# High and low parts in the MLP stages, and a reciprocal one step later, in an eight-stage transformer kernel

## The chip, the cores and the metric

The kernel runs on one core of one Trainium2 chip. The metric is the device time of one execution in microseconds, as the median of several executions.

## The reference

The reference is a chain of four transformer layers on x of 8 batches x 512 tokens x 256 features, with a second tensor (the context) of the same size. The kernel runs it as eight stages: causal self-attention, cross-attention and MLP (layer 0), cross-attention (layer 1), masked self-attention, cross-attention and MLP (layer 2), and causal attention with 64-wide heads (layer 3). The change touches the two MLPs and, by a step, the five attention stages with 16 heads of 16.

```
h = _ln(x, ln3_g, ln3_b)
h = jax.nn.gelu(_lin(h, fc_w, fc_b), approximate=False)   # 256 -> 1024
x = x + _lin(h, proj_w, proj_b)                           # 1024 -> 256
...
q = q.reshape(B, T, NUM_HEADS, HEAD_DIM)                  # attention, 16 heads of 16
scores = jnp.einsum('bqhd,bkhd->bhqk', q, k) * SCALE
probs = jax.nn.softmax(scores, axis=-1)
out = jnp.einsum('bhqk,bkhd->bqhd', probs, v).reshape(B, T, C)
```

All inputs and outputs are float32.

## The kernel before

The five engines each have a program of their own, written out by hand; they meet only in semaphores. x stays in SBUF as X, 128 tokens x 256 features per tile, four tiles for each of the eight batches. The stages run in the order SELF0, CROSS0, MLP0, CROSS1, SELF2, CROSS2, MLP2, SELF3.

**An MLP stage** (mlp(s) on each engine) goes over the eight batches. VectorE takes the statistics of the next batch's rows (layer_norm_x), and GpSimd makes the normalised rows XH from them (rows_scale, rows_centre, rows_times: four instructions) and later adds the output bias to X (add_bias). TensorE turns XH into the PSUM banks LA and LB (turn), and ScalarE moves them with scale and shift into hT (turned): features on partitions, 512 tokens. Then TensorE makes the eight chunks of 128 hidden features, each from two products (c = 0, 1) of a 128x128 piece of the first weights with hT (512 columns), in the four banks FR (the banks MX and ST in the trace). ScalarE puts each through Gelu into h1T (shown as V). After the eighth, TensorE turns the next batch, and then makes the output: for each of four tiles of 128 tokens, eight products of a 128x128 piece of h1T with 256 columns of the second weights, in the banks OV. VectorE adds these to X (add_to_x). All matmul operands of the MLP are plain float32; the trace has two records for each such matmul. The middle six batches are a hardware loop (Fori).

**The attention stages** go over 16 units each (a unit is a batch with 8 of the 16 heads). A unit is 8 steps i of 4 sub-steps j, written out in run_slots and slot. In each sub-step TensorE makes one tile of the row maxima of the next unit (max_tile, in the banks MX0, MX1 and OV1) and one tile of the scores of this unit (score_tile). Their operands come from stk, which already holds high and low parts of q and k in the type float32r, the rounded form that TensorE takes in one pass; each such matmul has one record. VectorE reduces each tile of maxima, in order, and frees its bank (mx_red). ScalarE makes the exponentials (exp_tile). A stage with a mask (SELF2) goes by GpSimd and VectorE too (add_mask), and ScalarE's exponential of such a tile follows a step later (late_exp); there, GpSimd multiplies the outputs between the masks of step 4 and step 5.

The sums of the softmax come with the outputs of attention. They are moved by DMA from ovs to the small tile few; VectorE inverts them (invert, line 1181, called at line 1137); two more DMAs, which SyncE issues in spread_rows and widen, spread the result over sums; and GpSimd multiplies the outputs by it (line 1470). project_out on TensorE waits for that, in every second unit, at step (6, 2). These are the lines that hold the reciprocal's place:

```
if at == ((2, 3) if lagged(s, u) else (1, 3)) and on["tail"]:
    invert(U, 1 - half)
```

lagged is true for the units of SELF2 and for the first unit that follows it.

In the trace, a line number of a helper stands for all its callers: L527 is every matmul, L537 every turn of XH, L1106 add_to_x, L993 Gelu, L987 turned, L1087 and L1094 the statistics.

## Time and profile before

| | |
|---|---|
| median of 3 runs | 4442.07 us (4435.71 to 4443.62) |
| profiled execution, its own time | 4439.38 us |
| its span, from first to last instruction | 4437.7 us |
| mean granted TensorE clock | 0.936 |
| the two MLP stages | about 1178 to 1422 us and 3113 to 3357 us of the span |

An instruction's record runs from its start to its end. Records of TensorE overlap, because matmuls are pipelined, so the pace of a series is read from the distance between starts, not from the length of one record. "Idle before" is the time in which the engine had nothing to do ahead of the instruction, with the engine and line that ended it.

### The profile page before, as it was taken

To read this page: it belongs to the slowest core of one execution; us is meant where nothing else is said; L and a number is where in the kernel's file an instruction comes from. 1 tells how busy PE (TensorE), PEld (TensorE's weight loads), DVE (VectorE), ACT (ScalarE), POOL (GpSimd) and SP (SyncE) were. 2 spreads that over 40 slices of the span, in tenths; PEclk is the share of its full clock that TensorE was granted. 3 is DMA by queue.
4 is the path that set the end of the run, shared out by engine and by line. 5 is a ranking of instruction groups with operands and counts; after the bars stand their busy time and mean duration, and the time that the engine had idled before them with its cause. 6 is when DMAs were issued, how large, how long until landed. Compare 5 with 4: busy or idle time off the path is not lost. (4 is left out here: it accounts for less than half of the span.)

```text
span 4437.7 us, 63144 instructions
## 1 busy us (share of the span) xinstructions
PE 4074.3 (92%) x19794; PEld 1951.2 (44%) x19794; DVE 2527.6 (57%) x6511; ACT 2391.1 (54%) x5045; POOL 1643.8 (37%) x1661
## 2 busy tenths in 40 slices
PE   6888899999797899999999999998897999999998
PEld 2333333333365333333333333333564555555555
DVE  4555557777102677778999977774102444444443
ACT  2444446666321466667788876665222555555553
POOL 2323321111122111126777632111223666666664
PEclk7888889999799799998999999997998999999999
DMA  4333334443000444434333344432000000000000
GB/s 97 82 60 61 64 63 91 80 77 71 23 0 10 65 103 80 74 70 79 61 59 65 59 89 80 78 74 42 20 0 29 6 11 1 11 11 11 11 6 10
DMA packets 135468, 219.92 MB, mean 50 GB/s; under 512 B 42736, under 2 KB 45168, under 8 KB 133488
## 3 DMA queue, kind: packets, MB, share of 16 engines
q1 hardware_dynamic: 135152, 216.02, 24.9%
q8 instruction: 160, 2.62, 0.3%
q14 instruction: 156, 1.28, 0.1%
HBM read 59.69 MB, written 5.51 MB: 15 GB/s over the span
## 5 line engine op out<-in xcount | busy, mean ns | idle before, releaser
L962 ACT ACTIVATE Pr<-ST 128x512 f32<-128x512 f32 (+3 forms) x2220 | 1161.2, 560 | 895.6 <-PE ST L527 881.4
L527 PE MATMUL ST<-stk 50*128 50x512 f32 (+3 forms) x2560 | 1029.0, 464 | 105.3 <-ACT Pr L962 71.8
L1167 DVE TENSOR_REDUCE mx<-MX 128x1 f32<-128x512 f32 x1056 | 699.1, 683 | 233.2 <-PE MX L527 232.5
L527 PE MATMUL MX<-stk 48*128 48x512 f32 (+3 forms) x1760 | 740.2, 458 | 24.4 <-issue 11.8
L1545 POOL TENSOR_SCALAR Pr<-Pr,mx 128x128 f32<-128x128 f32 (+3 forms) x512 | 549.1, 1085 | 386.0 <-DVE mx L1307 386.0
L527 PE MATMUL OV<-Pr,V 128*32 128x512 f32 (+3 forms) x4784 | 646.6, 615 | 2.6 <-ACT Pr L962 1.5
L527 PEld LDWEIGHTS MX<-stk 48*128 48x128 f32 x1760 | 316.7, 194 | 569.6 <-DVE mx L1167 231.3
L527 PEld LDWEIGHTS ST<-stk 50*128 50x128 f32 x2560 | 428.8, 194 | 285.8 <-ACT Pr L962 205.4
L1418 POOL CAST mhl<-mx 128x16 fp32r<-128x16 f32 x160 | 31.6, 198 | 1100.4 <-DVE mx L1167 1055.0
L527 PE MATMUL OV<-stk 48*128 48x512 f32 (+3 forms) x800 | 364.5, 456 | 58.8 <-DVE mx L1167 44.3
L1167 DVE TENSOR_REDUCE mx<-OV 128x1 f32<-128x512 f32 x480 | 324.7, 676 | 54.7 <-PE OV L527 53.4
L527 PEld LDWEIGHTS OV<-stk 48*128 48x128 f32 x800 | 156.5, 196 | 333.5 <-DVE mx L1167 221.3
L1034 ACT ACTIVATE Pr<-MX,mx 128x128 f32<-128x128 f32 (+3 forms) x256 | 135.1, 528 | 265.1 <-DVE mx L1301 264.7
L1164 DVE CUSTOM_DVE_ANT_0 MX<-MX,later 128x128 f32<-128x128 f32 (+3 forms) x352 | 174.1, 511 | 174.4 <-PE MX L527 171.9
L1415 POOL TENSOR_TENSOR X<-X,brow 128x1024 f32<-128x1024 f32 (+1 forms) x56 | 132.2, 2361 | 378.3 <-DVE X L1106 378.3
L1106 DVE TENSOR_TENSOR X<-OV,X 128x512 f32 (+1 forms) x32 | 22.1, 691 | 428.0 <-PE OV L527 428.0
L1160 DVE CUSTOM_DVE_ANT_0 MX<-MX,W_even 128x512 f32<-128x512 f32 x352 | 242.8, 699 | 32.3 <-PE MX L527 30.2
L1316 DVE COPY PT<-OV 128x128 f32<-128x128 f32 (+3 forms) x256 | 125.6, 491 | 227.7 <-PE OV L809 227.7
L1496 POOL TENSOR_TENSOR Pr<-Pr,W_odd 128x512 f32<-128x512 f32 x172 | 219.8, 1281 | 88.6 <-ACT Pr L962 88.2
L1301 DVE CUSTOM_DVE_ANT_0 MX<-MX,sums 128x128 f32<-128x128 f32 (+3 forms) x256 | 126.9, 496 | 212.7 <-PE ST L527 207.5
L527 PE MATMUL OV<-W_even,V 128*128 128x256 f32 x1024 | 225.2, 381 | 1.6 <-ACT V L993 1.6
L1503 POOL TENSOR_SCALAR_AFFINE_SELECT Pr<-Pr 128x512 f32<-128x512 f32 x128 | 81.4, 636 | 381.6 <-ACT Pr L962 381.6
(141 smaller groups left out, 7230.9 us busy)
## 6 DMA issues: line engine op xcount, KB each, us to landing
stk<-hi SPq DMA_DIRECT2D x640, 128.0 KB, 4.2
stk<-lo SPq DMA_DIRECT2D x320, 128.0 KB, 4.0
misc<-misc SPq DMA_DIRECT2D x160, 128.0 KB
sums<-spread SPq DMA_DIRECT2D x80, 256.0 KB
misc<-in_ctx_t SPq DMA_DIRECT2D x24, 512.0 KB, 6.5
W_even<-in_w SPq DMA_DIRECT2D x4, 1024.0 KB, 5.0
W_even<-in_w SPq DMA_DIRECT2D x2, 2048.0 KB, 10.0
XH<-in_ctx_rows SPq DMA_DIRECT2D x8, 512.0 KB, 3.9
```

Of the source, the lines that this page charges most:

```text
L527: return nc.tensor.matmul(o, l, r, start=start, stop=stop)
L962: nc.scalar.activation(pr_buffer(s, u, i)[:, h, q0:S], ST[h % 2][:, q0:S], ACT.Copy if addmask else ACT.Exp).then_inc(ex_done, 2 if addmas ...
L1034: nc.scalar.activation(P3(qt, h)[:, 0:k_n], S3[h][t % 2][:, 0:k_n], ACT.Exp, bias=low3[:, qt, h:h + 1], scale=-1.0, accum_out=total3[:, qt ...
L1160: nc.vector.tensor_tensor_reduce(bank[:, :], bank[:, :], mask_q[:, qt, :], 1.0, -3.0e38, ALU.add, ALU.max, m).then_inc(mx_red, 1)
L1164: nc.vector.tensor_tensor_reduce(bank[:, 0:k_n], bank[:, 0:k_n], later0[:, S - k_n:S], 1.0, -3.0e38, ALU.add, ALU.max, m).then_inc(mx_red, 1)
L1167: nc.vector.tensor_reduce(m, bank[:, :], AX.X, ALU.max).then_inc(mx_red, 1)
L1301: nc.vector.tensor_tensor_reduce(bank, bank, later3[:, S - k_n:S], 1.0, 3.0e38, ALU.add, ALU.min, low3[:, qt, h:h + 1]).then_inc(low3_done, 1)
L1316: nc.vector.tensor_copy(to, TP3[1][:, 0:P * (qt + 1)].rearrange("p (k n) -> p k n", n=P)).then_inc(tp3_evac[1], 1)
L1415: nc.gpsimd.tensor_tensor(xt(b, 0, NT), xt(b, 0, NT), bias, ALU.add).then_inc(x_done, 1)
L1496: nc.gpsimd.tensor_tensor(tile, tile, mask_k[:, i % 4, :], ALU.add).then_inc(pool_masked, 1)
L1503: nc.gpsimd.affine_select(tile, tile, [[0, G], [1, P]], ALU.is_ge, 0.0, 0, -1).then_inc(cleared, 1)
L1545: nc.gpsimd.tensor_scalar(tile, tile, inv3[:, qt, h:h + 1], None, ALU.mult).then_inc(nm3_done, 1)
```

## The change

In both MLP stages each matmul operand is held as a high part (the float32 value rounded to float32r) and a low part (the rest), and each product is made as three: high by high, low weight by high, and high weight by low. ScalarE cuts the weights' high parts in eight pieces at the head of the stage (split_weights) and VectorE the low ones (weights_low). ScalarE writes the turned rows twice, as hi and as hT, and VectorE subtracts them into lo (low_turned). VectorE makes h1_hi and h1_lo from each Gelu chunk (split_hidden). The eight batches are written out, with no loop. In VectorE's queue of the attention stages the reciprocal stands one step later: after sub-step (2, 3) in place of (1, 3), and after (3, 3) in place of (2, 3) where lagged holds. The new tiles lie on SBUF that the MLP stages don't use otherwise (stk, misc, Pr). GpSimd's part of the MLP does the same work as before, without the loop.

```diff
+        w_hi = stk[:, 16:24, :].rearrange("p a n -> p (a n)")
+        w_lo = stk[:, 24:32, :].rearrange("p a n -> p (a n)")
+        misc_at, pr_at = hot + 4 * 18432, hot + 4 * 26624
+        h1_hi = nc.alloc_sbuf_tensor_at("h1_hi", [P, NF, S], F32R, offset=misc_at)
+        h1_lo = nc.alloc_sbuf_tensor_at("h1_lo", [P, NF, S], F32R, offset=pr_at)
...
 
             return W[s % 2][:, 512 * m:512 * m + 512].rearrange("p (c o) -> p c o", c=NC)
 
+
+        def weight_cut(k):
+
+            if k < 4:
+                return [(E * k + c * 1024, E) for c in range(NC)]
+            return [(2048 + 512 * (k - 4), 512)]
+
+        def w_part(w, cut):
+
+            at, n = cut[0]
+            if len(cut) == 2:
+                return w[:, 0:2048].rearrange("p (c o) -> p c o", c=NC)[:, :, at:at + n]
+            return w[:, at:at + n]
 
         def stages(u):
 
...
 
             def mlp(s):
                 m = MLP_NO[s]
-                wf = W[s % 2][:, 0:2048].rearrange("p (c o) -> p c o", c=NC)
-                wp = W[s % 2][:, 2048:4096].rearrange("p (f o) -> p f o", f=NF)
+                wf_hi, wf_lo = (w[:, 0:2048].rearrange("p (c o) -> p c o", c=NC) for w in (w_hi, w_lo))
+                wp_hi, wp_lo = (w[:, 2048:4096].rearrange("p (f o) -> p f o", f=NF) for w in (w_hi, w_lo))
 
                 def turn(b):
                     MB = NB * m + b
...
                         wait(pe, ml_evac, 2 * (MB - 1) + c + 1)
                         transpose_x(s, b, c, bank).then_inc(ml_full, 1)
 
-                def batch(b, more):
+                def batch(b):
                     MB = NB * m + b
-                    pe.wait_ge(ml_evac, 2 * (MB + 1))
+                    pe.wait_ge(ml_hi, 2 * (MB + 1))
                     for f in range(NF):
+                        cut = slice(P * f, P * f + P)
                         wait(pe, gelu_done, NF * MB + f - 3)
+                        if b == 0 and f % 2 == 0:
+                            pe.wait_ge(wf_hi_done, 8 * m + f // 2 + 1)
+                            pe.wait_ge(wf_lo_done, 8 * m + f // 2 + 1)
                         for c in range(NC):
-                            last = mm(FR[f % 4][:, :], wf[:, c, P * f:P * f + P], hT[:, c, :], c == 0, c == NC - 1)
+                            mm(FR[f % 4][:, :], wf_hi[:, c, cut], hi[:, c, :], c == 0, False)
+                            mm(FR[f % 4][:, :], wf_lo[:, c, cut], hi[:, c, :], False, False)
+                        if f == 0:
+                            pe.wait_ge(ml_lo, 2 * (MB + 1))
+                        for c in range(NC):
+                            last = mm(FR[f % 4][:, :], wf_hi[:, c, cut], lo[:, c, :], False, c == NC - 1)
                         last.then_inc(fc_full, 1)
-                    if more:
+                    if b + 1 < NB:
                         turn(b + 1)
-                    pe.wait_ge(gelu_done, NF * (MB + 1))
+                    if b == 0:
+                        pe.wait_ge(wf_hi_done, 8 * (m + 1))
+                        pe.wait_ge(wf_lo_done, 8 * (m + 1))
                     for j in range(2):
                         wait(pe, pr_evac, 2 * (MB - 1) + j + 1)
                         for t in range(2):
-                            tok = slice(P * (2 * j + t), P * (2 * j + t) + P)
+                            tok, bank = slice(P * (2 * j + t), P * (2 * j + t) + P), OV[j][:, E * t:E * t + E]
                             for f in range(NF):
-                                last = mm(OV[j][:, E * t:E * t + E], h1T[:, f, tok], wp[:, f, :], f == 0, f == NF - 1)
+                                if j == 0 and t == 0:
+                                    pe.wait_ge(h1_hi_done, NF * MB + f + 1)
+                                mm(bank, h1_hi[:, f, tok], wp_hi[:, f, :], f == 0, False)
+                                mm(bank, h1_hi[:, f, tok], wp_lo[:, f, :], False, False)
+                            for f in range(NF):
+                                if j == 0 and t == 0:
+                                    pe.wait_ge(h1_lo_done, NF * MB + f + 1)
+                                last = mm(bank, h1_lo[:, f, tok], wp_hi[:, f, :], False, f == NF - 1)
                         last.then_inc(pr_full, 1)
 
                 turn(0)
-                batch(0, True)
-                with pe.Fori(1, NB - 1) as b:
-                    batch(b, True)
-                batch(NB - 1, False)
+                for b in range(NB):
+                    batch(b)
 
             def layer3(s):
                 w_q = W[1][:, 0:2048].rearrange("p (c o) -> p c o", c=NC)
...
             def mlp(s):
                 m = MLP_NO[s]
 
+                def split_weights():
+
+                    act.wait_ge(w_in[s], 16)
+                    for k in range(8):
+                        cut = weight_cut(k)
+                        nc.scalar.activation(w_part(w_hi, cut), w_part(W[s % 2], cut), ACT.Copy).then_inc(wf_hi_done, 1)
+
                 def turned(b):
+                    MB = NB * m + b
                     for c, bank in enumerate((LA, LB)):
-                        act.wait_ge(ml_full, 2 * (NB * m + b) + c + 1)
+                        act.wait_ge(ml_full, 2 * MB + c + 1)
+                        nc.scalar.activation(hi[:, c, :], bank[:, :], ACT.Identity, **scale_shift(s, c)).then_inc(ml_hi, 1)
                         nc.scalar.activation(hT[:, c, :], bank[:, :], ACT.Identity, **scale_shift(s, c)).then_inc(ml_evac, 1)
 
-                def batch(b, more):
+                def batch(b):
                     for f in range(NF):
                         at = C_F + NF * m + f
                         act.wait_ge(fc_full, NF * (NB * m + b) + f + 1)
                         nc.scalar.activation(h1T[:, f, :], FR[f % 4][:, :], ACT.Gelu,
                                              bias=cols[:, at:at + 1]).then_inc(gelu_done, 1)
-                    if more:
+                    if b + 1 < NB:
                         turned(b + 1)
 
+                split_weights()
                 turned(0)
-                batch(0, True)
-                with act.Fori(1, NB - 1) as b:
-                    batch(b, True)
-                batch(NB - 1, False)
+                for b in range(NB):
+                    batch(b)
 
             def layer3(s):
                 def slot(u):
...
                                 statistics(NB * sn + bn, xt(bn, j), j)
                             if at == (1, 0) and norm is not None:
                                 combine(NB * sn + bn)
-                            if at == ((2, 3) if lagged(s, u) else (1, 3)) and on["tail"]:
+                            if at == ((3, 3) if lagged(s, u) else (2, 3)) and on["tail"]:
                                 invert(U, 1 - half)
                             if at in (((3, 1), (4, 2)) if half == 0 else ((2, 2), (4, 1))) and on["a"]:
                                 low_part(sa, U, half, int(i == 4))
...
             def mlp(s):
                 m = MLP_NO[s]
 
-                def batch(b, more):
-                    if more:
+                def weights_low():
+                    for k in range(8):
+                        cut = weight_cut(k)
+                        dve.wait_ge(wf_hi_done, 8 * m + k + 1)
+                        nc.vector.tensor_tensor(w_part(w_lo, cut), w_part(W[s % 2], cut), w_part(w_hi, cut).bitcast(F32),
+                                                ALU.subtract).then_inc(wf_lo_done, 1)
+
+                def low_turned(b):
+                    for c in range(NC):
+                        dve.wait_ge(ml_evac, 2 * (NB * m + b) + c + 1)
+                        nc.vector.tensor_tensor(lo[:, c, :], hT[:, c, :], hi[:, c, :].bitcast(F32), ALU.subtract).then_inc(ml_lo, 1)
+
+                def split_hidden(b, f):
+                    at = NF * (NB * m + b) + f
+                    dve.wait_ge(gelu_done, at + 1)
+                    nc.vector.tensor_copy(h1_hi[:, f, :], h1T[:, f, :]).then_inc(h1_hi_done, 1)
+                    dve.wait_ge(h1_hi_done, at + 1)
+                    nc.vector.tensor_tensor(h1_lo[:, f, :], h1T[:, f, :], h1_hi[:, f, :].bitcast(F32),
+                                            ALU.subtract).then_inc(h1_lo_done, 1)
+
+                def batch(b):
+                    if b + 1 < NB:
                         layer_norm_x(NB * s + b + 1, b + 1)
+                    for f in range(NF):
+                        split_hidden(b, f)
+                    if b + 1 < NB:
+                        low_turned(b + 1)
                     for j in range(2):
                         dve.wait_ge(pr_full, 2 * (NB * m + b) + j + 1)
                         add_to_x(b, j, OV[j][:, :].rearrange("p (t n) -> p t n", t=2), pr_evac)
 
                 layer_norm_x(NB * s, 0)
-                batch(0, True)
-                with dve.Fori(1, NB - 1) as b:
-                    batch(b, True)
-                batch(NB - 1, False)
+                weights_low()
+                low_turned(0)
+                for b in range(NB):
+                    batch(b)
 
             def scale_queries(s, w, scale):
```

## Rows read from the trace of the kernel before

**Rows 1.** Busy us by stage; columns PE, PEld, DVE, ACT, POOL, then PEclk, DMA, GB/s.
```profile
620.00:1186.00 566.00, 515.76 (x2691) 204.46 (x2692) 374.46 (x650) 344.91 (x644) 100.88 (x129) 0.93 0.37 73
1186.00:1434.00 248.00, 232.19 (x831) 153.57 (x829) 31.36 (x78) 56.20 (x81) 55.55 (x37) 0.97 0.01 4
...
1990.00:2560.00 570.00, 537.70 (x2574) 213.73 (x2572) 523.91 (x1383) 458.36 (x854) 396.92 (x361) 0.93 0.36 65
```

**Rows 2.** Timeline of PE, one MLP batch (start us, us, engine, line, op, tiles).
```profile
1247.12 3.60 PE L527 MATMUL MX<-hT,W_even 128*128 128x512 f32 x8
...
1260.85 0.60 PE L537 MATMUL LA<-ident,XH 128*128 128x128 f32 x4
...
1261.89 14.08 PE L527 MATMUL OV<-W_even,V 128*128 128x256 f32 x64
1275.80 0.59 PE L527 MATMUL MX<-hT,W_even 128*128 128x512 f32 x1
```

**Rows 3.** Timelines of rounded matmuls at full clock: weight loads, then two matmuls in line.
```profile
131.50 0.19 PEld L527 LDWEIGHTS MX<-stk 48*128 48x128 f32 x1
131.61 0.19 PEld L527 LDWEIGHTS OV<-stk 48*128 48x128 f32 x1
...
625.66 0.39 PE L527 MATMUL MX<-stk 48*128 48x512 f32 x1
625.89 0.39 PE L527 MATMUL OV<-stk 48*128 48x512 f32 x1
```

**Rows 4.** Timeline, all engines, start of the first MLP stage.
```profile
1177.74 1.40 DVE L1087 BATCH_NORM_STATS2 st<-X 128x6 f32<-128x256 f32 x4 [2.45 <-POOL X L1415]
...
1182.97 1.89 POOL L1409 TENSOR_TENSOR XH<-XH,rstd 128x1024 f32<-128x1024 f32 x1
...
1186.19 0.78 ACT L987 ACTIVATE hT<-LA,cols 128x512 f32<-128x512 f32 x1 [29.76 <-PE LA L537]
```

**Rows 5.** Groups by line and shape of the nearest work of VectorE and GpSimd.
```profile
L1253 DVE TENSOR_TENSOR Pr<-Pr,W_odd 128x2048 f32<-128x2048 f32 x1 | 2.3, 2292 | 0.0
L1219 DVE TENSOR_SCALAR W_odd<-W_odd 128x512 f32<-128x512 f32 x3 | 1.3, 420 | 0.0
L1106 DVE TENSOR_TENSOR X<-OV,X 128x512 f32 x24 | 16.6, 691 | 308.3 <-PE OV L527 308.3
L1415 POOL TENSOR_TENSOR X<-X,brow 128x1024 f32 x12 | 28.2, 2352 | 250.7 <-DVE X L1106 250.7
L1398 POOL TENSOR_TENSOR rstd<-rstd,mhalf 128x4 f32<-128x4 f32 x72 | 74.7, 1038 | 6.0
```

**Rows 6.** Timeline, first microseconds: VectorE's copies beside GpSimd's memset.
```profile
0.97 7.07 POOL L1579 MEMSET stk<- 32x4096 f32 x2
...
5.59 2.53 DVE L1352 CAST identr<-ident 128x128 fp32r<-128x128 f32 x1 [5.59 <-issue]
```

**Rows 7.** What PE waited for over the whole run (us in total, times, longest).
```profile
PE OV L527 <- DVE mx L1167: 44.3, 24, 4.6
...
PE OV L527 <- DVE mx L1164: 12.5, 7, 2.3
```

**Rows 8.** Timeline around one reciprocal of the first cross stage.
```profile
881.86 0.35 DVE L1181 RECIPROCAL few<-few 128x32 f32<-128x32 f32 x1 [2.91 <-DMA few<-misc]
...
889.78 1.28 POOL L1470 TENSOR_TENSOR misc<-misc,sums 128x512 f32<-128x512 f32 x1
...
899.07 1.13 PE L527 MATMUL LB<-W_odd,misc 128*128 128x256 f32 x4
```

**Rows 9.** Timeline of one unit of the masked stage: DVE, POOL, ACT.
```profile
2234.66 0.35 DVE L1181 RECIPROCAL few<-few 128x32 f32<-128x32 f32 x1
...
2243.75 1.28 POOL L1470 TENSOR_TENSOR misc<-misc,sums 128x512 f32<-128x512 f32 x1
2244.99 1.28 POOL L1496 TENSOR_TENSOR Pr_third<-Pr_third,W_odd 128x512 f32<-128x512 f32 x1
...
2248.52 1.13 ACT L972 ACTIVATE Pr_third<-Pr_third 128x512 f32<-128x512 f32 x2
```

More of the change, by code:

```diff
@@ L193, in program @@
             sem("fc_full"), sem("gelu_done"), sem("pr_full"), sem("pr_evac"), sem("ml_full"), sem("ml_evac"))
+        ml_hi, ml_lo, h1_hi_done, h1_lo_done = sem("ml_hi"), sem("ml_lo"), sem("h1_hi_done"), sem("h1_lo_done")
+        wf_hi_done, wf_lo_done = sem("wf_hi_done"), sem("wf_lo_done")
         bias3, later3_set, cols3_in, k3_apart = sem("bias3"), sem("later3_set"), sem("cols3_in"), sem("k3_apart")
@@ L1513, in mlp @@
                 m = MLP_NO[s]
-                def batch(b, more):
-                    if more:
+                layer_norm(NB * s, xt(0, 0, NT))
+                for b in range(NB):
+                    if b + 1 < NB:
                         layer_norm(NB * s + b + 1, xt(b + 1, 0, NT), ml_full, 2 * (NB * m + b + 1))
@@ L1519, in batch @@
                     add_bias(s, b)
-                layer_norm(NB * s, xt(0, 0, NT))
-                batch(0, True)
-                with pool.Fori(1, NB - 1) as b:
-                    batch(b, True)
-                batch(NB - 1, False)
             def layer3(s):
```

## The prediction

> **What bounds the kernel now.** I read the table of windows first, with one window for each stage. In the MLP stages TensorE is busy in 232 of 248 us, at a granted clock of 0.97 of 2.4 GHz, while VectorE has 31, ScalarE 56 and GpSimd 56 us of work [rows 1]: TensorE is the bound, and there is much room beside it. In the cross stages TensorE is busy in 516 of 566 us and VectorE in 374; in the masked stage VectorE has 524 of 570 [rows 1]. Then the timeline of one MLP batch on TensorE: it lasts 1275.80 - 1247.12 = 28.68 us, of which the hidden chunks take 13.73 (to 1260.85), the turn of the next batch and a short wait 1.04, and the output products 13.91 [rows 2]. Those are 16 and 32 float32 matmuls, so 0.86 us for 512 columns and 0.43 for 256. Last the list of waits: TensorE stood still before its tile of maxima in the bank OV for 44.3 us in the cross stages (24 times) and 12.5 us in the causal one (7 times) [rows 7]. One such place shows why. VectorE sits 2.91 us in front of the reciprocal, because the DMA that fills few has not landed [rows 8]; the reductions queued behind it free no bank, so TensorE stops about 1.85 us later on (44.3 / 24).
>
> **The change, part by part.** All sums are against the profiled execution, 4439.4 us, with 1.7 us around its span; the median is 2.7 us higher.
>
> *TensorE in the MLP.* Removed are 48 float32 matmuls per batch, added 144 rounded ones: 48 of 512 columns and 96 of 256. Two rounded matmuls of 512 columns in line start 625.89 - 625.66 = 0.23 us apart at full clock [rows 3], so the hidden chunks take 48 x 0.23 = 11.04 us. No row shows 256 columns in line. Half of 0.23 is 0.115, and weight loads follow each other at 0.11 [rows 3], beside the matmuls; I take 0.115, with 0.11 and 0.12 as ends. The output products take 96 x 0.115 = 11.04 us (10.6 to 11.5). The turn is 1.04 less its wait for the last Gelu, 0.87, for the output can start on the first chunk. A batch is 22.95 us, which is 5.73 less than 28.68; 16 batches give -91.7 us.
>
> The Trainium skill (TensorE: Matmul & The Clock Gate, "Back-to-back issue gap") gives N / 2.4 + 2.5 ns, or 0.216 us for 512 columns, as an isolated gap. The row shows 0.23, so I stay with it; by the page's figure the estimate would be some 1.3 us per batch lower.
>
> *The head of the stage.* ScalarE's eight copies of weights (at most 8 x 0.78, by its move of a bank of the same size) start when X is ready, at 1177.7, and end before the first turned rows at 1186.19 [rows 4], so they are hidden. Two of the four moves of turned rows are new; TensorE now waits for three of them, not two: +0.78 per stage. ScalarE's later two moves per batch lie beside the output products. VectorE's eight subtractions end long before TensorE needs them, but the statistics of batch 1 are now queued behind them and behind low_turned, so they come at about 1190 instead of 1179.5; GpSimd then needs some 6 us and the turn of batch 1 is due at about 1200. That is covered; each microsecond that they came later than some 3 would cost one. Sum +1.6 us.
>
> *VectorE beside GpSimd.* This is the term I am least sure of. A subtraction of 512 columns: a quarter of the 2.29 us that 2048 take is 0.57 from below, and the addition from PSUM took 0.69 from above [rows 5]; I take 0.62. The rounding copy: 0.42 by the scaled weights [rows 5], with its wait 0.45, and 0.69 at most. Sixteen of these per batch are 8 x 1.07 = 8.6 us, under the 11.04 us in which the chunks come, so by itself VectorE keeps up: the last low part is there at about 12.9 us of the batch and is wanted at 11.04 + 0.87 + 23 x 0.115 = 14.6. But in the first microseconds a rounding copy of only 128 columns took 2.53 us and ended at 8.12, just behind GpSimd's memset, which ended at 8.04 [rows 6]. A copy in SBUF waited for a whole GpSimd instruction. In each batch GpSimd runs 2.35 (bias), a small 0.23, 1.04 and twice 1.90 us [rows 4, 5], starting at about 1.0 us; VectorE begins its splitting at 2.7, after the addition to X and the statistics. If the two take strict turns, 5.7 us of GpSimd and 8.6 of VectorE with 0.3 of gaps lie between 2.7 and 17.3, and the last low part is 2.8 us late. TensorE stops for that in the 14 batches that have a next one: +39 us. At the head of a stage GpSimd's normalisation and the cutting of weights take turns too, four turns of about 0.6 us: +5 us in two stages. Bounds: 0 if they never meet, and with 0.69 for both operations 8 x 1.38 = 11.0 in place of 8.6, so 2.4 us later still, 14 x 5.2 + 5 = +78. I take +44, since the one row that shows the two side by side shows a full wait.
>
> The Trainium skill (SBUF — State Buffer, "SBUF: two separate sides") says that VectorE and GpSimd share one port pair as an exclusive lock, held for a whole instruction, by a VectorE instruction in a 2-port mode or with two SBUF inputs. The copy in the trace agrees; no row shows the subtraction beside GpSimd.
>
> *The reciprocal.* Between the old and the new place VectorE has four reductions that follow TensorE's pace, about 3.5 to 4 us, more than the 2.91 us of the wait [rows 8]; in the causal stage TensorE's longest stop was 2.3 us [rows 7], and a rest may stay. So the stalls of rows 7 go, 44.3 + 12.5 = 56.8 us, of which I count nine tenths: -51. The granted clock is 0.93 in the cross stages [rows 1]; some dips to 1.2 GHz follow the stalls, and I add -6 (0 to -15). What is moved with it: SyncE's two DMAs for spreading, the DMAs of the next q and k behind them in its queue (wanted only in the next unit, some 15 us on), and GpSimd's multiplication. There the output product comes at 899.07 and the multiplication at 889.78 to 891.06 [rows 8], so 8 us of room. In the masked stage VectorE doesn't wait, so nothing is won, and the reciprocal comes about 4.5 us later in truth. The chain from reciprocal to multiplication takes 7.9 us [rows 8], against 9.1 us there [rows 9], so GpSimd waits 2 to 4 us in front of the masks of step 5. Its first mask ends at 2246.3 and ScalarE takes its tile at about 2249 [rows 9]: 2.2 to 2.8 us are covered, and up to 1.5 us per unit get through. I take 0.4 x 15 = +6 us (0 to +22).
>
> *Sum*: -91.7 + 1.6 + 44 - 51 - 6 + 6 = -97. 4439.4 - 97 = 4342, and 4345 as a median.
>
> **The rivals.**
> *The port costs nothing worth naming.* The subtractions may not be held, or VectorE may win the port. For it: the row shows only a copy beside a long memset, and 17 of 23 us would suffice for both engines. Then +44 falls away: about 4300.
> *The port costs the whole gain of the MLP.* GpSimd's normalisation is late as well, or the rounding copy takes 0.69 us: TensorE waits at the turn or for the parts, and a batch stays near 28 us. Against it: 0.42 us for a scaled copy. Result: 4442 - 51 or about 4390.
> *The reciprocal only moves its wait.* The multiplication and ScalarE's tiles in the masked stage pay what the other stages win, or TensorE's place is taken by another wait. Against it: the 2.91 us end with the landing, which doesn't depend on VectorE. Only the MLP's -46, with +20: about 4415.
> *Weight loads that don't hide, the slower side.* Each rounded matmul has a load of its own, 144 per batch where float32 had 96, and half as many columns to hide one behind. If 0.09 us of a load stayed bare, 144 x 16 x 0.09 = 207 us would come on top, less the hidden 44: about 4510. It decides from (91.7 + 51) / 2304 = 0.06 us bare per matmul on. Against it: loads at 0.11 us in line with matmuls between them [rows 3].
>
> **How the numbers follow.** Forecast 0.50, port free 0.23, port eats the MLP's gain 0.12, reciprocal wins nothing 0.09, bare loads 0.06. The forecast's own range is 4320 to 4370. The range of 4285 to 4410 takes in the free port with its low ends (0.11 us per matmul, the clock) and the eaten gain; the last two stay out, with tails of the others. A difference of 0.2%, 9 us, is about what can be told from no change. Faster 0.93, the same 0.02, slower 0.05; the fourth case is still faster.
>
> **What the profile after would show.** A batch of the MLP of 23 us (port free), 26 (forecast) or 28 (eaten), read between the first chunks of two batches; rounded matmuls 0.23 and 0.115 us apart; TensorE idle before an output product, released by VectorE's h1 parts; copies or subtractions of VectorE, or GpSimd's 1.90 us instructions, with records up to twice as long; no idle time of VectorE before the reciprocal, and the 56.8 us of waits near 5; in the masked stage a wait of GpSimd before line 1470's multiplication. The prediction is wrong if the pace of the 256-column products is over 0.13 us, or if the cross stages keep their length.

## The result, and the profile after

The kernel after takes 4280.01 us (median of 4 runs, 4268.74 to 4284.06), the kernel before in the same rounds 4438.89: a ratio of 0.9641, 95% interval 0.9615 to 0.9667. The prediction was 4345, with a range from 4285 to 4410. So the direction was right; the time came out 65 us under the forecast, 5 us beyond the low end of the range.

Stages first. The table of windows, each from the last addition to X of one stage (VectorE) to that of the next, for the kernel after: first cross stage, first MLP stage, masked stage. It answers to [rows 1], whose windows are rounder: its 566 us for the cross stage begin 62 us before the stage does.

```profile
658.30:1123.20 464.90, 442.34 (x2387) 174.72 (x2386) 329.27 (x565) 309.92 (x575) 81.18 (x104) 0.96 0.45 77
1123.20:1331.70 208.50, 192.39 (x1216) 173.47 (x1216) 136.65 (x232) 71.24 (x105) 67.89 (x40) 0.97 0.02 7
...
1930.80:2502.80 572.00, 539.00 (x2632) 218.18 (x2632) 527.86 (x1344) 461.61 (x867) 391.52 (x359) 0.96 0.42 66
```

The same cut of the kernel before gives 493.3, 244.7 and 580.4 us. Both MLP stages together went from 489.5 to 418.1 us, 71.4 less, and all the rest from 3948.2 to 3848.9, 99.3 less. The prediction had 46 and 51. The surprise is in the attention stages: 682.0 to 658.3 us (the first), 493.3 to 464.9, 621.3 to 599.1, 580.4 to 572.0 (masked), 488.7 to 468.1, and 1082.5 to 1086.5 in the last, which the change doesn't touch. Two of these are uncertain: in a second profile of the same kernel (e11_after_again, below) the first stage took 650.2 us and the masked one 586.0, the other attention stages within 4 us of the first profile but for the last (1082.0).

Next one MLP batch. The timeline of TensorE in the kernel after; it answers to [rows 2].

```profile
1162.23 1.09 PE L547 MATMUL MX<-hi,stk 128*128 128x512 f32 x4
1163.16 0.62 PE L547 MATMUL MX<-lo,stk 128*128 128x512 f32 x2
1163.62 1.07 PE L547 MATMUL MX<-hi,stk 128*128 128x512 f32 x4
...
1173.15 0.60 PE L557 MATMUL LA<-ident,XH 128*128 128x128 f32 x4
...
1176.66 0.51 PE L547 MATMUL OV<-stk,h_hi 128*128 128x256 f32 x2 [0.56 <-DVE h_hi L1262]
...
1177.96 2.08 PE L547 MATMUL OV<-stk,h_hi 128*128 128x256 f32 x16
...
1180.84 2.08 PE L547 MATMUL OV<-stk,h_hi 128*128 128x256 f32 x16
...
1186.60 1.09 PE L547 MATMUL MX<-hi,stk 128*128 128x512 f32 x4
```

A batch takes 1186.60 - 1162.23 = 24.37 us for 28.68. The eight chunks start 1.36 us apart past the first, 0.227 for each of six matmuls. A tile of 24 output products takes 1180.84 - 1177.96 = 2.88, which is 0.12 each. TensorE stops once, before its products with the last h1_hi part, which VectorE makes.

The list of waits of TensorE for the whole run answers to [rows 7]. The two rows for bank OV are gone; this is what is left for maxima:

```profile
PE MX L547 <- DVE mx L1211: 3.7, 5, 2.1
...
PE MX L547 <- DVE mx L1204: 1.0, 6, 0.2
```

And one reciprocal of the cross stage with its multiplication and output product, which answers to [rows 8]. No idle time stands behind the reciprocal any more, the idle time now stands with GpSimd (4.44 us), and the product has 3.5 us of room behind the multiplication's end at 915.30, where it had 8.

```profile
906.21 0.34 DVE L1225 RECIPROCAL few<-few 128x32 f32<-128x32 f32 x1
...
914.02 1.28 POOL L1538 TENSOR_TENSOR misc<-misc,sums 128x512 f32<-128x512 f32 x1 [4.44 <-DMA sums<-spread]
...
918.78 1.13 PE L547 MATMUL LB<-W_odd,misc 128*128 128x256 f32 x4
```

### The profile page after: what moved, and what is told of

The parts are those of the page before. It is cut to its first block and busy times, and to the rows that moved or that the text cites. A ratio compares the mean times of both kernels' runs of the same rounds, so it can differ in the third digit from the quotient of the medians.

```text
span 4267.0 us, 64410 instructions
## 1 busy us (share of the span) xinstructions
PE 3949.2 (93%) x20562; PEld 1985.0 (47%) x20562; DVE 2756.7 (65%) x6815; ACT 2414.2 (57%) x5093; POOL 1660.3 (39%) x1661
## 3 DMA queue, kind: packets, MB, share of 16 engines
q8 instruction: 176, 2.88, 0.3%
## 5 line engine op out<-in xcount | busy, mean ns | idle before, releaser
L547 PE MATMUL ST<-stk 50*128 50x512 f32 (+3 forms) x2560 | 1006.6, 456 | 104.5 <-ACT Pr L998 75.8
L547 PE MATMUL OV<-Pr,V 128*32 128x512 f32 (+3 forms) x4784 | 633.7, 603 | 2.9 <-ACT Pr L998 1.5
L547 PE MATMUL OV<-stk 48*128 48x512 f32 (+3 forms) x800 | 355.3, 444 | 0.1
L1483 POOL TENSOR_TENSOR X<-X,brow 128x1024 f32<-128x1024 f32 x56 | 133.0, 2375 | 276.6 <-DVE X L1150 276.6
L1538 POOL TENSOR_TENSOR misc<-misc,sums 128x512 f32<-128x512 f32 x80 | 102.3, 1279 | 302.9 <-DMA sums<-spread 302.9
L1008 ACT ACTIVATE Pr<-Pr 128x512 f32<-128x512 f32 x344 | 205.2, 627 | 18.4 <-POOL Pr L1564 18.3
```

Source lines behind the costliest of these rows:

```text
L547: return nc.tensor.matmul(o, l, r, start=start, stop=stop)
L1008: nc.scalar.activation(tile, tile, ACT.Exp).then_inc(late_done, 1)
L1483: nc.gpsimd.tensor_tensor(xt(b, 0, NT), xt(b, 0, NT), bias, ALU.add).then_inc(x_done, 1)
```

## The experiments

Times are medians. The runs came in three groups: e1, e2, e5 and e6, beside which the kernel before took 4440.4 us; e3, e4, e7 and e8, beside 4433.7; and e9, e10 and e11, beside 4447.2. The ratios are against the kernel before of the same group. "Lost to the clock" is one minus the mean granted clock, times the span: 284 us in the profile before, 239 in the one after. It counts time in which TensorE has nothing to do as well, so it is an upper bound for what the clock costs; TensorE's busy time for the same instructions is the stricter measure.

### Each half alone

```diff
# e1_products_alone, on the kernel after
-  if at == ((3, 3) if lagged(s, u) else (2, 3)) and on["tail"]:
+  if at == ((2, 3) if lagged(s, u) else (1, 3)) and on["tail"]:
# e2_reciprocal_alone: the opposite edit on the kernel before
```

> The kernel after with the reciprocal back at its old two places (one step earlier in VectorE's queue): the three-product MLP stages alone. Theory A (the traces: the MLP stages became 71 us shorter, the attention stages 103 us): 71 us under the kernel before, 4368, ratio 0.984, MLP stages of 208 to 210 us and cross stages of 478 and 472 us again. Theory B (the prediction's sum: 92 us of TensorE less 44 us for VectorE beside GpSimd, +2 us): 46 us less, 4393. Theory C (the attention stages gained from the new MLP stages too, by how the stages join or by TensorE's clock): over 100 us less, under 4340.

> The kernel before with only the reciprocal of a unit's sums moved one step later. Theory A (the stage lengths of the two traces): 103 us less, about 4336, ratio 0.977; each cross stage shorter by 22 to 32 us, the first part by 20, the masked stage by 8; TensorE's 1.2 GHz stretches in the cross stages gone. Theory B (the prediction's term: nine tenths of the 56.8 us of waits for maxima, and 6 us of clock, less 6 us in the masked stage): 51 us less, about 4388. Theory C (the reciprocal's move gives nothing by itself, its wait only moves): within 10 us of 4439.

Measured: e1_products_alone 4377.4 us, ratio 0.9846 (0.9806 to 0.9886); e2_reciprocal_alone 4348.2, ratio 0.9780 (0.9744 to 0.9817). 63 and 92 us add up to 155 of the 159 that both give. The MLP stages of the first are 209.6 and 208.4 us long and its cross stages 493.4 and 495.0, against 493.3 and 488.7 in the kernel before, so nothing clear of noise passes between the halves, and its theory A holds within the interval (the 478 and 472 us that it names for the cross stages are not by this cut). For the second, theory A (4336) lies in the interval, theories B (4388) and C do not. It has the same 19794 matmuls as the kernel before, so its page can be set beside that one's. The busy row, first of the kernel before:

```profile
PE 4074.3 (92%) x19794; PEld 1951.2 (44%) x19794; DVE 2527.6 (57%) x6511; ACT 2391.1 (54%) x5045; POOL 1643.8 (37%) x1661
```

and of e2_reciprocal_alone:

```profile
PE 4033.7 (93%) x19794; PEld 1947.2 (45%) x19794; DVE 2531.5 (58%) x6511; ACT 2384.5 (55%) x5045; POOL 1643.3 (38%) x1661
```

TensorE's waits for maxima fell from 60.9 us (five rows) to 5.0, and its busy time by 40.6 for the same instructions. Together 96.5, and the span fell by 94.3. The waits are the -51 of the prediction. The busy time is TensorE's clock: the loss went from 284 to (1 - 0.944) x 4343.4 = 243 us. Over all executions the median loss is 285 us for the kernel before and 246 for this one.

### Where the clock goes

In the trace of the kernel before, one stop at a reciprocal, by TensorE's timeline:

```profile
882.81 0.50 PE L527 MATMUL OV<-stk 48*128 48x512 f32 x1 [1.69 <-DVE mx L1167]
```

and by the table of windows around it (PEclk is the third column from the right):

```profile
876.00:880.00 4.00, 4.00 (x26) 1.39 (x22) 2.94 (x9) 2.42 (x5) 2.58 (x3) 1.00 1.11 126
880.00:884.00 4.00, 2.31 (x14) 0.67 (x6) 2.14 (x5) 2.50 (x5) 2.48 (x2) 1.00 0.17 25
884.00:888.00 4.00, 4.00 (x17) 1.01 (x16) 2.43 (x5) 1.09 (x3) 0.00 (x0) 0.57 0.18 66
888.00:892.00 4.00, 4.00 (x21) 1.25 (x19) 3.44 (x6) 3.25 (x7) 2.60 (x4) 1.00 0.49 98
```

TensorE works 2.31 of 4 us, and in the next 4 us its granted clock is 0.57, which is mostly the level of 1.2 GHz. The stop is paid twice. Not every stop is: the stage has eight such stops of 1.7 to 2.0 us, and before its last 60 us the clock falls at 755, 820 and 885 us only. But each of these three falls stands at a stop; the other two are

```profile
754.53 0.57 PE L527 MATMUL OV<-stk 48*128 48x512 f32 x1 [1.72 <-DVE mx L1167]
...
819.45 0.63 PE L527 MATMUL OV<-stk 48*128 48x512 f32 x1 [1.77 <-DVE mx L1167]
```

and the kernel after has in the same part of the stage (658 to 1075 us) no such stop and not one fall. A series on the reciprocal's place tells whether the loss follows the stops:

```diff
# on the kernel after, the place of invert(U, 1 - half)
# e10_reciprocal_earlier       ((2, 1) if lagged(s, u) else (1, 1))
# e8_reciprocal_half_step      ((3, 1) if lagged(s, u) else (2, 1))
# e4_reciprocal_two_later      ((4, 3) if lagged(s, u) else (3, 3))
# e11_after_again              no edit
```

> The kernel after with the reciprocal two tiles earlier than in the kernel before, four steps of a series (two earlier, as before, two later, four later as in the kernel after). VectorE's wait for the DMA grows by about 2 us in each unit, to 3.5 and 5 us in the cross stages. Theory A (TensorE's clock is lost with its stops: 42.5 us of clock went with 56.8 us of waits): of 2 us in each of 64 units some 110 to 130 us of stops come back on top, and 40 to 80 us of clock; the clock lost (one minus the granted clock, by the span) rises from 285 to 330 or more, time 4377 + 150 to 200: about 4540. Theory B (the clock doesn't follow the stops): the stops come, the lost clock stays at 285 to 300, about 4490.

> The kernel after with the reciprocal two tiles later than in the kernel before, where the kernel after has it four tiles later. VectorE was idle 1.5 us in front of it in one unit of the cross stages and 3.0 us in the next, a tile of its queue is about 1 us. Theory A (waits of TensorE for maxima and its clock go together: what the shorter wait no longer costs is also not paid in stretches at 1.2 GHz): waits for maxima in OV of 5 to 15 us for 56.8 and 0, TensorE busy 5 to 15 us more than in the kernel after, 10 to 30 us slower: 4290 to 4310. Theory B (the clock's 40 us come from something else that the move does, not from the waits): waits gone but TensorE's busy time anywhere, with time between 4280 and 4330 not following the waits.

> The kernel after with the reciprocal moved one more step later (two steps from its place in the kernel before). The trace after shows no idle time of VectorE in front of it any more, so there is nothing left to take from VectorE; the spread of the sums over the partitions, GpSimd's multiplication and the output product come about 4 us later. Theory A (the output product has slack): within 5 us of the kernel after, 4275 to 4290. Theory B (the sums are late: GpSimd waits 4 us more in front of a mask, a clear or the bias addition, and TensorE after it): 30 to 80 us more, 4310 to 4360, with a wait of TensorE or VectorE behind GpSimd.

> The kernel after, unchanged, on the same chip and in the same rounds as the two others, so that they can be compared with it. 4280 by its runs so far (4269 to 4284); its profile is a second look at where the clock is lost, which was 239 us in the first.

| place, tiles later than before | kernel | time | span (profile) | TensorE's waits for maxima | TensorE busy | lost to the clock |
|---|---|---|---|---|---|---|
| -2 | e10_reciprocal_earlier | 4550.2 | 4544.4 | 163.1 | 4073.1 | 400 |
| 0 | e1_products_alone | 4377.4 | 4375.7 | 64.6 | 3997.8 | 298 |
| 2 | e8_reciprocal_half_step | 4288.9 | 4291.8 | 12.8 | 3969.1 | 258 |
| 4 | after | 4280.0 | 4267.0 | 4.7 | 3949.2 | 239 |
| 4 | e11_after_again | 4271.1 | 4273.1 | 4.7 | 3951.4 | 248 |
| 8 | e4_reciprocal_two_later | 4348.4 | 4350.1 | 2.0 | 3975.6 | 283 |

The waits are sums over the rows of the list of waits that name maxima. From place 4 back to 0 they rise by 60 and the busy time by 49; from 0 to -2 by another 98 and 75, and the span by 169. Over these two intervals each microsecond of stop costs 1.7 to 1.8 of the span, and stops and busy time together make up nearly all of it (108.5 for 108.7 us, and 173.8 for 168.7). Theory A of the two first holds: between places -2 and 4 the same 20562 matmuls lose 124 us of busy time, in step with the stops, while their MLP stages keep a clock of 0.96 to 0.97. The first cross stage shows it by itself, first at place 0 (the kernel before), then at place -2:

```profile
682.00:1175.30 493.30, 457.20 (x2387) 179.02 (x2386) 328.34 (x565) 311.05 (x575) 80.75 (x104) 0.93 0.37 72
```

```profile
704.20:1246.90 542.70, 478.10 (x2387) 183.54 (x2386) 329.31 (x565) 312.44 (x575) 80.60 (x104) 0.88 0.34 66
```

At place 4 it has 0.96 (above). In its numbers theory A missed: 98 us of added stops where I had 110 to 130, and 102 us of lost clock where I had 40 to 80 (of which 75 are busy time); at place 2, 20 us more busy time where I had 5 to 15. One unit each, from the timelines of VectorE and TensorE in e10_reciprocal_earlier and of VectorE in e8_reciprocal_half_step:

```profile
920.30 0.35 DVE L1225 RECIPROCAL few<-few 128x32 f32<-128x32 f32 x1 [4.12 <-DMA few<-misc]
...
921.26 0.79 PE L547 MATMUL MX<-stk 48*128 48x512 f32 x1 [3.89 <-DVE mx L1211]
```

```profile
913.72 0.35 DVE L1225 RECIPROCAL few<-few 128x32 f32<-128x32 f32 x1 [1.70 <-DMA few<-misc]
```

Idle times of VectorE of 0 (the kernel after), 1.70, 2.91 (the kernel before) and 4.12 us went with stops of TensorE of 0, 0, 1.69 and 3.89 us. A short wait is covered; above that the stop grows faster than the wait. Longer stops also take the clock more surely: in that stage of e10_reciprocal_earlier all eight stops of 3.9 to 4.8 us have a stretch at the 1.2 GHz level beside them, and of the six of 1.6 to 2.6 us only two.

A single profile is a rough measure of the lost clock, for it varies between executions of one kernel: 270 to 317 us in eleven of the kernel before, 239 to 266 in the first four of the kernel after (239 is its profile, the fastest of them) and 225 to 248 in the next five. The medians over the executions of each row, from place -2 to 8, are 404, 293, 258, 254, 248 and 287 us, so the order of the table stands. The 8 us of stops and 19 to 25 us of span between places 4 and 2 are too small to give a price.

Place 8 was meant as a test of the slack, and theory B is right: 4348 us, all of the loss in one stage. The masked stage grows from 572.0 (586.0 in the second profile) to 654.0 us, the others stay within 6 us. The waits in that stage, of GpSimd, ScalarE and TensorE, in e4_reciprocal_two_later:

```profile
POOL misc L1538 <- DMA sums<-spread: 131.5, 16, 10.6
```

```profile
ACT Pr L1008 <- POOL Pr L1564: 64.2, 15, 6.4
ACT Pr_third L1008 <- POOL Pr_third L1564: 32.7, 8, 6.1
```

```profile
PE ST L547 <- ACT Pr L998: 22.7, 15, 4.5
```

In the kernel after the same rows say 58.5, 18.3, 11.6 and 5.3. This is the chain that the prediction costed at 0 to 22 us for one step: GpSimd stands in front of its multiplication, the masks queue behind it, ScalarE gets its tiles late. One step already brings some of it (no row of the kernel before has ScalarE waiting there for GpSimd's masks), without a clear loss; at two the cover is gone.

### The masked stage at its old place

```diff
# e3_masked_early, on the kernel after
-  if at == ((3, 3) if lagged(s, u) else (2, 3)) and on["tail"]:
+  if at == (2, 3) and on["tail"]:
```

> The kernel after, but in the 15 or 16 units of the masked stage the reciprocal stays at its old place (behind step 2's work); everywhere else it is one step later. Theory A (the prediction: GpSimd's multiplication then waits for the late sums in front of the masks of step 5, the trace after shows 3 to 4.5 us of it in each of these units, and part of it reaches TensorE): 6 us less than the kernel after, about 4274, up to 15 less. Theory B (the trace after: the masked stage is 4 to 8 us shorter than before although VectorE had no idle time in front of its reciprocals there): 4 to 8 us more, about 4286. Theory C (that stage's gain comes from its neighbours' units alone): no difference, within 3 us.

Measured: 4267.7 us, ratio 0.9625 (0.9592 to 0.9659), beside 0.9641 and 0.9593 for two groups of runs of the kernel after. The masked stage took 577.1 us, and 572.0 and 586.0 in the two profiles of the kernel after. The stage varies by 14 us without an edit, so this can't be told apart. The term is small; its sign stays open.

### The port between VectorE and GpSimd

The timeline of VectorE and GpSimd in the batch shown above, kernel after:

```profile
1164.63 1.25 DVE L1262 CAST h_hi<-V 128x512 fp32r<-128x512 f32 x1
...
1165.92 0.69 DVE L1264 TENSOR_TENSOR h_lo<-V,h_hi 128x512 fp32r<-128x512 f32 x1
1166.06 1.45 POOL L1466 TENSOR_TENSOR rstd<-rstd,mhalf 128x4 f32<-128x4 f32 x1
...
1166.53 0.42 DVE L1262 CAST h_hi<-V 128x512 fp32r<-128x512 f32 x1
...
1167.59 2.18 POOL L1472 TENSOR_TENSOR XH<-X,mv 128x1024 f32<-128x1024 f32 x1
...
1168.05 2.27 DVE L1264 TENSOR_TENSOR h_lo<-V,h_hi 128x512 fp32r<-128x512 f32 x1
...
1169.85 2.22 POOL L1477 TENSOR_TENSOR XH<-XH,rstd 128x1024 f32<-128x1024 f32 x1
...
1170.24 2.12 DVE L1262 CAST h_hi<-V 128x512 fp32r<-128x512 f32 x1
```

Three instructions of VectorE are held: 1.25 for 0.42, 2.27 for 0.69, 2.12 for 0.42 us, 4.1 us in all, each to 0.3 to 0.6 us past the end of a GpSimd instruction of 1024 columns. GpSimd's are stretched as well (2.18 and 2.22 for 1.90). But beside the power instruction on 4 columns (1.45 us) VectorE's run at full pace, here and in all 14 batches that have one; there it is GpSimd that waits (1.45 for 1.04, and 0.40 for 0.23 in the scaling before it).

```diff
# e6_gpsimd_short, on the kernel after, GpSimd in the MLP stages
-  tensor_tensor(XH[:, :, :], rows, mv[:, :, 0:1].broadcast_to([P, NT, E]), ...)
+  tensor_tensor(XH[:, :, 0:2], rows[:, :, 0:2], mv[:, :, 0:1].broadcast_to([P, NT, 2]), ...)
...
# e5_high_by_scalar, on the kernel after: ScalarE, then VectorE
+  nc.scalar.activation(h1_hi[:, f, :], FR[f % 4][:, :], ACT.Gelu, bias=...).then_inc(h1_hi_done, 1)
   nc.scalar.activation(h1T[:, f, :], FR[f % 4][:, :], ACT.Gelu, bias=...).then_inc(gelu_done, 1)
...
-  nc.vector.tensor_copy(h1_hi[:, f, :], h1T[:, f, :]).then_inc(h1_hi_done, 1)
-  dve.wait_ge(h1_hi_done, at + 1)
```

e6_gpsimd_short leaves 254 of 256 columns unnormalised and without bias, so its output is wrong; it is there for the time alone.

> The kernel after, with GpSimd's normalisation and bias addition in the MLP stages cut to 2 of 256 columns of each row (the rest of the rows is left unnormalised and without bias), so that GpSimd hardly works beside VectorE there. Theory A (VectorE's splitting is late only because of GpSimd): a batch of 23.0 us for 24.4, 7 x 2 x 1.4 = 20 us less, and the heads of the stages up to 5 us shorter: 4255 to 4262. Theory B (the splitting is late by its own length, 8 x 1.1 us in order behind the Gelus and behind the row statistics): the batch keeps its 24.4 us, 4275 to 4285.

> The kernel after, with the high part of the hidden layer written by ScalarE from the PSUM bank (its Gelu is run twice, once into each tensor), so that VectorE has 8 copies of 0.42 us less in each batch; ScalarE has 8 Gelus of about 0.7 us more. Theory A (what is left of the port's price in a batch, 1.2 to 1.5 us of TensorE before the output product, is VectorE's copies and subtractions beside GpSimd): 0.8 to 1.3 us less in 14 of 16 batches, 11 to 18 us under the kernel after, 4262 to 4269. Theory B (ScalarE is late instead: 16 Gelus of 0.7 us and 4 evacuations in a batch of 23 us leave it free, but each chunk's bank is freed 0.7 us later): no gain or up to 10 us more, 4280 to 4290.

Measured: e6_gpsimd_short 4251.8 us (0.9567, 0.9531 to 0.9604), e5_high_by_scalar 4260.5 (0.9580, 0.9544 to 0.9616). The timeline of TensorE, two first chunks in line, for the one:

```profile
1156.24 1.09 PE L547 MATMUL MX<-hi,stk 128*128 128x512 f32 x4
...
1179.55 1.09 PE L547 MATMUL MX<-hi,stk 128*128 128x512 f32 x4
```

and for the other:

```profile
1165.49 1.09 PE L547 MATMUL MX<-hi,stk 128*128 128x512 f32 x4
...
1188.79 1.09 PE L547 MATMUL MX<-hi,stk 128*128 128x512 f32 x4
```

Both batches take 23.3 us: 48 x 0.227 + 0.87 + 96 x 0.12. So the stop for h1_hi is 24.37 - 23.30 = 1.07 us. By VectorE's last additions to X of each batch it is in 6 batches of 8 per stage, 12.8 us in all. Theory A holds in both, each time a few us under its numbers. The MLP stages of e6_gpsimd_short are 19.8 us shorter than the kernel after's, of which some 7 are no port: its GpSimd also normalises the first batch faster, while TensorE waits for it.

### What is next in the MLP

```diff
# e7_two_products, on the kernel after
-  mm(FR[f % 4][:, :], wf_lo[:, c, cut], hi[:, c, :], False, False)
...
-  mm(bank, h1_hi[:, f, tok], wp_lo[:, f, :], False, False)
```

> The kernel after without the products of the weights' low parts in the MLP stages (two products of three; the splitting of the weights stays): the output lacks these terms. Theory A (TensorE's instructions set a batch's length): 16 matmuls of 0.227 us and 32 of 0.12 us less in each of 16 batches, 7.5 us each, 119 us less: 4161. Theory B (VectorE's copies and subtractions beside GpSimd, some 14 us of it in a batch, are next and already close): the batch stops at 18 to 19 us, 80 to 95 us less: 4185 to 4200.

Measured: 4227.7 us (0.9520, 0.9479 to 0.9561), 52 less than the kernel after's 4280.0 in another group, so both theories missed. Its output lacks the terms of the weights' low parts. A batch takes 21.35 us, in 4 of 12 22.84, where TensorE's instructions need 32 x 0.227 + 0.87 + 64 x 0.12 = 15.8. Two rows of TensorE's list of waits (the first had 69.3 us in 4 waits after):

```profile
PE LA L557 <- POOL XH L1475: 103.8, 16, 27.9
...
PE OV L547 <- DVE h_hi L1260: 28.7, 45, 0.7
```

The first is the larger, some (103.8 - 69.3) / 12 = 2.9 us at the turn of a batch, for GpSimd's normalised rows. But the second ends last, as the timeline of one batch shows (VectorE and TensorE):

```profile
1164.97 0.63 PE L547 MATMUL MX<-hi,stk 128*128 128x512 f32 x2
1165.17 0.69 DVE L1148 TENSOR_TENSOR X<-OV,X 128x512 f32<-128x512 f32 x1 [3.13 <-PE OV L547]
...
1174.95 1.09 PE L557 MATMUL LA<-ident,XH 128*128 128x128 f32 x4 [2.54 <-POOL XH L1475]
...
1178.92 0.42 DVE L1260 CAST h_hi<-V 128x512 fp32r<-128x512 f32 x1
1179.39 0.39 PE L547 MATMUL OV<-stk,h_hi 128*128 128x256 f32 x1 [0.68 <-DVE h_hi L1260]
...
1186.32 0.63 PE L547 MATMUL MX<-hi,stk 128*128 128x512 f32 x2
```

I had counted engines' work. The limit is a loop through two engines: VectorE's last addition to X, its statistics and its splitting with the holds by GpSimd, 14.2 us from the addition's start to the end of the last high part (1179.34 - 1165.17); then what TensorE has left behind that part, 6.9 us (1186.32 - 1179.39), the end of which releases the next addition. In the kernel after the first part of the loop is 14.2 us too (1176.61 - 1162.43) and the second 9.9 (1186.60 - 1176.66). The difference, 3.0 us, is the 25 products of 0.12 us that stand behind the last high part there and not here, and it is the whole gain of a batch (24.37 - 21.35); the other 23 products that are left out buy nothing. So theory B of this run named the right engine and left out what TensorE does behind it. The turn alone would allow a batch of some 19 us (an estimate: 1176.5 for the first output product, 64 x 0.12, less 1164.97). The stops cost clock as well: the two MLP stages are granted 0.91 and 0.89, for 0.97 and 0.96 in the kernel after. With three products the turn isn't waited for: its rows are ready at 1172.07, 1.1 us before TensorE wants them.

### A version that is faster than both

```diff
# e9_scalar_high_masked_early: the edits of e5_high_by_scalar and e3_masked_early together
```

> The two edits that each looked no worse than the kernel after, together: ScalarE writes the high part of the hidden layer (18 us less in the profiled run's MLP stages: 418 to 405 is 13 us), and the reciprocal stays at its old place in the masked stage. Theory A (they add, and the masked stage costs 5 us but the medians of the whole kernel showed 4268 for 4280): 4250 to 4258, ratio 0.957. Theory B (the masked stage's reciprocal is worth 5 us where it is in the kernel after): 4265.

Measured: 4251.5 us (4249.3 to 4255.8), ratio 0.9556 (0.9534 to 0.9578), beside 4271.1 (4255.2 to 4274.8) and 0.9593 for the kernel after in the same rounds. It is 0.5% faster. By its batches of 23.30 us ScalarE's high parts carry 13 us of the 20; the rest is no more than the noise of the clock. So theory A has the number, but that the masked edit adds anything isn't shown.

## Why the prediction was off, by its own steps

| step | predicted | measured |
|---|---|---|
| TensorE in the MLP | -91.7 | -86: 16 x (28.68 - 23.30) |
| head of the stages, with GpSimd there | +1.6 + 5 | about +3.5 |
| VectorE beside GpSimd in the batches | +39 | +12.8 |
| waits for maxima | -51 | -56 |
| clock | -6 (0 to -15) | -41 alone, -45 in the whole; by medians of all executions -39 and -31 |
| masked stage | +6 | not told from 0 |
| sum | -97 | about -167; spans -170.7; median times -158.9 |

**The step that failed first is the clock.** "Some dips to 1.2 GHz follow the stalls, and I add -6 (0 to -15)": it was 41 us, as much again as three quarters of the waits. The -6 had no working behind it, neither a price per stop nor a total. The total stood in the table of the kernel before: a mean granted clock of 0.936 is 284 us lost of 4437.7. What share was in play could have been bounded by the stages' PEclk, 0.93 in the cross stages against 0.97 in the MLP [rows 1]; over the 2866 us of attention before the last stage the whole step of 0.04 is 115 us, and half of it 57. With a bound at either the range would have held the result.

**The second is the size of the port's price.** The +39 in the batches was +12.8. The mechanism was right, and its sign: VectorE's records are up to five times as long (I had said twice), TensorE stops before an output product, released by h1_hi. Strict turns were wrong. Of GpSimd's 7.4 us in a batch only the instructions of 1024 columns held VectorE, for 4.1 us; the two on 4 columns did not. So VectorE ended its splitting at 1177.3, 15.1 us into the batch, where I had 17.3. And what TensorE stops for is the last high part, at 14.4 us, which it wants at about 13.4; I had looked at the last low part, wanted at 14.6. The Trainium skill (SBUF — State Buffer, "SBUF: two separate sides") calls the shared port pair an exclusive lock for a whole instruction, taken by a VectorE instruction in a 2-port mode or, against a GpSimd instruction that reads SBUF, by one with two SBUF inputs. The trace agrees for the long ones: a subtraction with two SBUF inputs took 2.27 for 0.69 us. It does not for the short: a copy and a subtraction of VectorE took their usual 0.42 and 0.69 within the 1.45 us of the power instruction.

**What held.** The chunks' pace was 0.227 for 0.23, the output products' 0.12, the upper of my two ends for 0.115; that is the 5.6 us by which the first term was too good. The loads stayed hidden: 0.12 us per pair leaves no room for the 0.06 us at which the slower rival decides. The waits went entirely. The rival "port free" gave 4300, nearest to the result but not for its reason; "the port costs the whole gain" is refuted by the batch of 24.37 us, and "the reciprocal only moves its wait" by e2_reciprocal_alone.

Both errors had one sign, 35 and 26 us of the 70 between the two sums; the small terms nearly cancel. (The profile of the kernel after is its fastest execution; by the median it is 65.) The range's low end held the free port, but of the clock only 15 us.

## What to carry to other kernels

Where a stop of TensorE can be taken away, price it with the clock as well: here each microsecond of stop cost 1.7 to 1.8 of time, between places -2, 0 and 4 of a series. Read the lost clock of the whole run, and of each stage, before the places are looked at singly. A wait can be moved later only as far as its result has cover, and the stage with the least cover decides: one step was worth 92 us, and a second gave back 68 to 82 of the span in the masked stage alone. When a bound engine's work is cut, look for the dependence chain that is just under it, not for the next engine's sum: here VectorE's 14.2 us and what TensorE has left behind them. Of several waits in a batch the one that ends last sets its length, not the longest.

## What was not expected of the hardware

- A GpSimd instruction on 4 columns doesn't hold VectorE's copies and subtractions, one on 1024 columns does, until just past its end: 0.42 to 2.12 us and 0.69 to 2.27.
- Matmuls of rounded float32 with a weight load each run at 0.227 us for 512 columns and 0.12 for 256 at 2.4 GHz.
- The granted clock fell to the 1.2 GHz level behind a stop of 1.69 us, but behind only three of eight of its kind, and beside all eight stops of 3.9 to 4.8 us. Which of the short ones it follows is not settled by these runs; the sum over many is.
